# Rows of the input and output laid two neighbours to a partition, in pieces of 2 KB

## The reference, cut to what matters

```
# x: (64, 256, 256), ctx_768: (64, 120, 192), all float32
def xattn(q, kv, Wq, Wk, Wv, Wo, bo):            # 8 heads of 32
    scores = einsum('bqhd,bkhd->bhqk', heads(q @ Wq), heads(kv @ Wk)) * 32 ** -0.5
    out = einsum('bhqk,bkhd->bqhd', softmax(scores), heads(kv @ Wv))
    return out @ Wo + bo

def ffn(x, g1, b1n, w1, b1, g2, b2n, w2, b2):    # 256 -> 1024 -> 256
    h = bitlinear(layernorm(x, g1, b1n), w1, b1) # each row rounded to 8 bits by its own
    h = gelu(h)                                  # largest magnitude, weights to -1, 0, 1
    return bitlinear(layernorm(h, g2, b2n), w2, b2)

x = x + xattn(layernorm(x), ctx_768, ...)
x = x + ffn(layernorm(x), ...)
```

## Time and profile before

| What | Value |
|---|---|
| Median of three runs | 1029.75 us |
| Profiled execution, own time | 1027.94 us |
| Span of the profiled execution | 1026.3 us |
| PE busy | 919.9 us (90%) |
| DVE busy | 915.6 us (89%) |
| ACT busy | 931.9 us (91%) |
| POOL busy | 776.1 us (76%) |
| Mean granted TensorE clock | 0.977 |
| DMA packets | 276079, 146.98 MB |

### The profile page before, as it was taken

One profiled execution on the slowest core, in us unless ns is written; L12 is line 12 of the kernel. 1 busy time (PEld: TensorE's weight loads), 2 busy tenths in 40 slices (PEclk: granted clock), 3 DMA queues, 4 the chain that ended last, 5 costly groups with the idle time before them and its releaser, 6 DMA issues.

```text
span 1026.3 us, 25999 instructions
## 1 busy us (share of the span) xinstructions
PE 919.9 (90%) x7410; PEld 558.2 (54%) x7442; DVE 915.6 (89%) x1192; ACT 931.9 (91%) x2667; POOL 776.1 (76%) x1189
## 2 busy tenths in 40 slices
PE   6999999999999999999999868888888888888886
PEld 4666666666666666666666413344444444444434
DVE  2588888888888888888888899999999999999996
ACT  4789999999999999999997888999999999999993
POOL 3266665777666666666667687999999999999997
PEclk9999999999999999999999956999999999999998
DMA  6589987777866566666665333877777777777787
GB/s 171 149 158 202 185 172 164 170 158 171 173 171 153 169 163 168 162 157 175 163 161 134 94 82 69 123 125 123 121 122 121 124 120 123 121 122 123 123 124 120
DMA packets 276079, 146.98 MB, mean 143 GB/s; under 512 B 183320, under 2 KB 266520, under 8 KB 276016
## 3 DMA queue, kind: packets, MB, share of 16 engines
q1 hardware_dynamic: 258432, 129.29, 57.5%
q0 software_dynamic: 16864, 16.26, 13.3%
q10 hardware_dynamic: 720, 0.66, 0.2%
HBM read 71.62 MB, written 33.63 MB: 103 GB/s over the span
## 4 chain that ended last, share of the span: by engine, by line
PE 54%; DVE 16%; issue 14%; POOL 6%; ACT 5%; DMA 2%; SPq 1%; ACTq 1%; DVEq 0%; POOLq 0%
PE banks L1386 11%; PE banks L1377 10%; PE banks L1298 6%; PE banks L1350 6%; DVE g_max L861 6%; PE banks L1339 5%; DVE gn_low L849 4%; PE banks L1370 4%; PE banks L1360 3%; POOL nq L594 2%; DVE gn_high L849 2%; PE banks L1328 2%; PE banks L1266 2%; PE banks L1364 2%; DVE gn_high L835 2%
## 5 line engine op out<-in xcount | busy, mean ns | idle before, releaser
L1232 PE MATMUL banks<-w_t,h_t 128*128 128x512 bf16 x473 | 130.7, 399 | 81.6 <-DVE gn_low L835 39.1
L751 DVE TRANSPOSE_TENSOR_REDUCE nm_part<-banks 128x64 f16<-128x2048 f32 x64 | 147.7, 2307 | 2.6 <-PE banks L1298 2.2
L1089 ACT ACTIVATE banks<-banks,h_dq 128x1024 f32<-128x1024 f32 x128 | 141.6, 1106 | 8.3 <-PE banks L1237 6.3
L1095 ACT ACTIVATE g_dev<-banks,g_sum 128x1024 bf16<-128x1024 f32 x128 | 145.8, 1139 | 0.0
L1042 ACT ACTIVATE probs<-banks 120x512 f32<-120x512 f32 x256 | 132.2, 603 | 13.8 <-PE banks L1328 10.3
L1266 PE MATMUL banks<-w_t,g_t 128*128 128x256 bf16 x1024 | 136.8, 278 | 5.4 <-ACT h L1128 4.7
L1386 PE MATMUL banks<-wo_sb,o_t 128*128 128x256 f32 x512 | 135.2, 399 | 1.2 <-DVE xr L757 0.8
L1266 PEld LDWEIGHTS banks<-w_t,g_t 128*128 128x128 f16 x1024 | 92.8, 99 | 55.1 <-issue 39.0
L1232 PEld LDWEIGHTS banks<-w_t,h_t 128*128 (+1 forms) x504 | 48.1, 99 | 136.6 <-issue 99.1
L1377 PE MATMUL banks<-xt,wq_c 128*128 128x256 f32 x512 | 121.7, 381 | 0.0
L536 POOL COPY h_dq<-h_cl 128x2 f32<-128x2 f32 (+1 forms) x64 | 12.0, 188 | 140.8 <-DVE h_qs L814 137.8
(11 more groups left out here) (170 smaller groups left out, 2526.9 us busy)
## 6 DMA issues: line engine op xcount, KB each, us to landing
x_in<-in_x SPq DMA_DIRECT2D x64, 256.0 KB, 4.8
xt<-in_x_t SPq DMA_DIRECT2D x64, 256.0 KB, 4.1
xr<-in_x SPq DMA_DIRECT2D x64, 256.0 KB, 4.3
out<-xr SPq DMA_DIRECT2D x64, 256.0 KB, 6.0
out<-h POOLq DMA_DIRECT2D x62, 256.0 KB, 5.0
ctx_t<-in_ctx_t SPq DMA_DIRECT2D x64, 128.0 KB, 3.9
r_bc<-r_rows SPq DMA_DIRECT2D x63, 128.0 KB, 4.1
w_raw<-in_w_t SPq DMA_DIRECT2D x8, 256.0 KB, 6.1
```

The lines of the kernel that those rows point to most:

```text
L751: dve.tensor_reduce(nm_part[:, :, 0:C * RB], blocks_p, AX.X, ALU.max, negate=True, apply_transpose=True).then_inc(max_done, 1)
L1089: act.activation(u_p[t], u_p[t], ACT.Gelu, scale=h_dq[:, b, t:t + 1], accum_out=g_sum[:, p, t:t + 1]).then_inc(gelu_done, 1)
L1095: act.activation(g_dev[:, t, :], u_p[t], ACT.Square, scale=-float(F), bias=g_sum[:, p, t:t + 1], accum_out=g_ssq[:, p, t:t + 1]).then_inc( ...
L1232: pe.matmul(u_p[t][:, cols], h_t[:, b, t * C + c, :], w1_t[:, c, cols], start=(c == 0), stop=False, skip_group_check=True)
```

## The change

Five DMAs that move rows of a batch, and the host's layout of the turned input, take another order of the rows. Partition p now holds rows 2p and 2p + 1, row 2p + t in tile t. In memory these two rows are neighbours, so what was two pieces of 1 KB for a partition, 128 KB apart, is one piece of 2 KB. The turned input gives the columns in the same order. The last stores, of one tile each, still move pieces of 1 KB, now every second row.

```
-x_in[:, q, :, :] <- x[b].rearrange("(t p) n -> p t n", p=P)          # L405
+x_in[:, q, :, :] <- x[b].rearrange("(p t) n -> p t n", p=P)
-xr[:, r, :, :] <- x[b].rearrange("(t p) n -> p t n", p=P)            # L417
+xr[:, r, :, :] <- x[b].rearrange("(p t) n -> p t n", p=P)
-out[b].rearrange("(t p) n -> p t n", p=P) <- xr[:, r, :, :]          # L421
+out[b].rearrange("(p t) n -> p t n", p=P) <- xr[:, r, :, :]
-out[b].rearrange("(t p) n -> p t n", p=P)[:, t, :] <- res[...]       # L442
+out[b].rearrange("(p t) n -> p t n", p=P)[:, t, :] <- res[...]
-out[b].rearrange("(t p) n -> p t n", p=P) += res[:, r, :, :]         # L585
+out[b].rearrange("(p t) n -> p t n", p=P) += res[:, r, :, :]
...
 def laid_out(inputs):
-    a["x_t"] = a["x"].transpose(0, 2, 1).reshape(nb, d // P, P, rows).transpose(0, 2, 1, 3)
+    tiles = a["x"].reshape(nb, P, rows // P, d).transpose(0, 2, 1, 3).reshape(nb, rows, d)
+    a["x_t"] = tiles.transpose(0, 2, 1).reshape(nb, d // P, P, rows).transpose(0, 2, 1, 3)
```

More of the change, by code:

```diff
@@ L404, in attn @@
                         after(sp, x_ssq, (b - 1) * T)
-                        sp.dma_start(x_in[:, q, :, :], x[b].rearrange("(t p) n -> p t n", p=P)).then_inc(x_loaded[q], 16)
+                        sp.dma_start(x_in[:, q, :, :], x[b].rearrange("(p t) n -> p t n", p=P)).then_inc(x_loaded[q], 16)
                     b = i + 3
@@ L416, in attn @@
                         after(sp, x1_stored[r], (b - r) * 4)
-                        sp.dma_start(xr[:, r, :, :], x[b].rearrange("(t p) n -> p t n", p=P)).then_inc(xr_loaded[r], 16)
+                        sp.dma_start(xr[:, r, :, :], x[b].rearrange("(p t) n -> p t n", p=P)).then_inc(xr_loaded[r], 16)
                     b, r = i - 4, n
@@ L420, in attn @@
                         sp.wait_ge(b2_done, b + 1)
-                        sp.dma_start(out[b].rearrange("(t p) n -> p t n", p=P), xr[:, r, :, :]).then_inc(x1_stored[r], 16)
+                        sp.dma_start(out[b].rearrange("(p t) n -> p t n", p=P), xr[:, r, :, :]).then_inc(x1_stored[r], 16)
                     b = i + 3
@@ L441, in store_last @@
                     sp.wait_ge(last_out, count)
-                    sp.dma_start(out[b].rearrange("(t p) n -> p t n", p=P)[:, t, :], res[:, b % 4, t, :]).then_inc(last_stored, 16)
+                    sp.dma_start(out[b].rearrange("(p t) n -> p t n", p=P)[:, t, :], res[:, b % 4, t, :]).then_inc(last_stored, 16)
                 for n, b in enumerate((NB - 2, NB - 1)):
@@ L584, in store @@
                     pool.wait_ge(out_done, b * T + T)
-                    pool.dma_start(out[b].rearrange("(t p) n -> p t n", p=P), res[:, r, :, :],
+                    pool.dma_start(out[b].rearrange("(p t) n -> p t n", p=P), res[:, r, :, :],
                                    accum_op=ALU.add).then_inc(stored[r], 16)
```

## The result

The changed kernel takes 1033.38 us (median of 20 runs, 1029.58 to 1041.84), the kernel before on the same chip 1028.76 (20 runs): a ratio of 1.0046, 95% interval 1.0032 to 1.0060. It is slower by about 4.6 us. The forecast was 1029.0 in a range of 1025.5 to 1032.0. The profiled execution took 1033.8 us, with a span of 1032.1; rows of a profile are always of one execution.

A forecast was written before the change was run, and what follows sets the result against it. It took PE to bound the attention half and DVE the feed forward half. -0.6 (140 to 302 us) - 0.1 (start) + 0 = -0.7 us from the median 1029.75 gave 1029.05, predicted as 1029.0, range 1025.5 to 1032.

The forecast's parts named there:

- The packets: Whole kernel: packets fall from 276,079 to 243,567, of which 201,496 are under 2 KB.
- Rival 2: Whole kernel: pieces don't become 2 KB, packets stay at 276,079 and time at 1029.75 us; chance 0.06.
- What is steady: Both halves' steady parts wait for no DMA; batch periods stay at 8.75 and 6.44 us.
- rival 4: Feed forward half: adding pieces of 2 KB at 483 ns make DMA the bound, +19 us, 1049; chance 0.05.
- The adding store on POOL: Feed forward half: issue falls from 1.26 to 1.1 us, the saving turns into L619's wait for ACT; gain 0.
- The last store: Kernel end: the 3.6 us store keeps 1 KB pieces; taken as 0, bounds -0.3 to +1.4 us.
- Rival 3: Between the halves: earlier loads close PE's gaps, up to 7.6 us of clock loss goes, 1021.5; chance 0.07.
- The plain transfers: Loads and stores of rows: each lands 0.1 us sooner, bounds 0 and 0.7; counts only where a transfer sets the end.
- The start: First loads: chain passes 5.40 us through a weight load; gain 0.1 us, bounds 0 and 0.7.
- The stretch from 140 to 302 us: Attention half: 2.4 us lost in the chain through the small store; 0.6 comes back, bounds 0 and 2.4.

The follow-up runs named there:

- e1: The changed kernel again, nothing edited: 1032.29 us, ratio to the kernel before 1.0026 (1.0007 to 1.0045).
- e3: The kernel before with only the loads x_in and xr in pieces of 2 KB: 1033.77 us, ratio to the kernel before 1.0033.
- e4: The changed kernel with the small store of the deviations issued ahead of the attention store: 1031.08 us, ratio to the kernel before 1.0021.
- f1: The kernel before with x_in alone in pieces of 2 KB: 1034.50 us, ratio to the kernel before 1.0014 (0.9983 to 1.0044).
- g0: The changed kernel again, nothing edited, on another chip: 1032.57 us, ratio to the kernel before 1.0039 (1.0021 to 1.0056).
- g2: The changed kernel with the three broadcast loads behind r_bc near 24 us issued a step later: 1033.29 us, ratio to the kernel before 1.0030.
- e2: The kernel before with only the attention store to out in pieces of 2 KB: 1027.46 us, ratio to the kernel before 0.9983.
- f2: The kernel before with xr alone in pieces of 2 KB: 1033.54 us, ratio to the kernel before 0.9983 (0.9959 to 1.0006).
- f3: The changed kernel with x_in's tile padded, so its load has pieces of 1 KB: 1034.24 us, ratio to the kernel before 0.9987.
- f4: The changed kernel with x_in padded and xr loaded as two DMAs, 2 KB pieces in stores alone: 1032.64 us, ratio to the kernel before 0.9981.
- g3: The changed kernel with all loads in 1 KB and whole-batch stores in 2 KB, as f4, on another chip: 1028.95 us, ratio to before 1.0006.
- h1: The kernel before with r_bc loaded from 128 different rows of x: 1030.84 us, ratio to the kernel before 0.9963 (0.9940 to 0.9986).
- k1: The kernel before with the small store of the deviations ahead of the attention store: 1033.93 us, ratio to the kernel before 1.0007.
- k2: The changed kernel with loads in 1 KB, whole-batch stores in 2 KB, small store ahead of the attention store: 1031.97 us, ratio to before 0.9972.
- h3: The changed kernel with r_bc issued ahead of the context and the turned rows: 1078.25 us, ratio to the kernel before 1.0418.
- h4: The kernel before with r_bc issued ahead of the context and the turned rows: 1080.26 us, ratio to the kernel before 1.0444.
- g1: The changed kernel with r_bc loaded from 128 different rows of x: 1030.11 us, ratio to the kernel before 1.0014 (0.9997 to 1.0032).

## Why the prediction was wrong

*The packets*: right, 243,567 with 201,496 under 2 KB. Rival 2 is out.

*What is steady*: right. From 302 us on no batch of the attention half is longer (all start 5.4 us later than before), the feed forward half takes 1032.1 - 605.2 = 426.9 us against 426.5, and the DMA share of 0.68 instead of 0.63 cost nothing. That also puts an end to rival 4: the adding queue holds 0.124 x 16 x 1032.1 / 8928 = 229 ns for a packet, at most 258 for a data piece of 2 KB, where I took 250 and the rival needed 443.

*The adding store on POOL*: right in kind. The issue fell from 1.26 to 0.94 us (and is 0.94 in every kernel with this store in 2 KB); I took 1.1. In 300 us that saves 283.1 - 267.7 = 15.4 us of POOL, and L619's wait for ACT rose by 15.4, from 4.4 to 19.8. All of it went into the wait, as forecast. The rule cited from the Trainium skill, "DMA: Bandwidth & Descriptors", "Anatomy of one DMA — SWDGE (gpsimd) path", would have left the issue at 1.26 us. The measurement decides against it here: half as many descriptors took a quarter off.

*The last store*: right, 1028.67 to 1032.1 is 3.4 us, against 3.6.

*Rival 3*: the clock between the halves didn't recover; the first five batches there take 645.5 - 605.2 = 40.3 us against 39.8. The clock did move the time, but at 34 us, and downwards.

*The plain transfers*: this is the step that failed: "The bounds are therefore 0 and 0.7 us for each transfer". It failed twice. It bounded a larger piece only on the side of the gain, while the adding piece and the last store had got a bound on both sides. Measured by the median landing, `x_in` gained 0.1 us (4.8 to 4.7), as taken, `xr` lost 0.1 (4.3 to 4.4) and the attention store lost 0.7 (6.0 to 6.7). And it bounded the changed transfer by itself, from there to "the chain there consists of landings of 5 to 7 us which do not change themselves but wait behind x_in, xr and out. If each falls by 0.1". The landings behind them did not fall. Near 24 us `r_bc`, 1 KB for each partition like before, lands after 4.6 to 6.5 us in the seven profiled executions with `x_in` in 2 KB, the small array as source and an unchanged queue up to there (after, e1, e3, e4, f1, g0, g2), and after 2.9 to 3.8 in the nine with `x_in` in 1 KB (before, e2, f2, f3, f4, g3, h1, k1, k2). Its packets divide in the same way, 96 to 109 ns against 48 to 72. Where L413 itself was moved, it is 5.1 in h3 and 3.9 in h4, with 1 KB. (The expectation of f1 counts three late profiles and gives 3.7 for one of the others; e4 was a fourth, and the kernel before has 3.1.) The three steps overlap a little, 28.0 to 31.1 us against 27.5 to 28.5, because of e4 and k2.

So the record shows that `x_in` in 2 KB goes with the late `r_bc`, and that this costs 1.7 to 3.5 us at the start in six of seven executions and 0.5 in one. That it also takes the small array as source is shown by g1 for this place (27.5 us). Whether it is the one shared row or that it was written just before, and how it works together with the pieces of `x_in`, is not shown. It may be that with larger pieces all engines come to the shared row at the same moment; this is argued, not measured.

The start was also named in the prediction as a place where a transfer can set the end, but for its first chain link of 5.40 us, and with a gain only. DVE's idle time of 4.66 us ahead of 27.46 was there to be read: the same wait had a second releaser close behind, for `r_bc` had landed at 23.7 + 3.1 = 26.8 us, 0.7 us before DVE's start. A landing 2.7 us later could not be hidden.

*The stretch from 140 to 302 us*: forecast -0.6 us with bounds of 0 and -2.4. From the fourth batch to the end of this stretch it was +2.5 (2.9 us behind at the fourth, 5.4 at the end), of which 2.4 had come by 142.2 us before and 147.5 after, the fifteenth batch: the larger part lies before 140 us, where I had not looked; the DMA share from 85 to 190 us was 0.89 before. The mechanism was named rightly (SP's queue behind the small store), the direction wrongly. How much of these 2.5 us comes from the change stays open. Over the twelve steps from the tenth batch the changed kernel takes 4.8 us more than 12 x 8.75, the kernel before 2.1. On one chip g0 and g2, with the changed loads and the shared row, lose 6.3 and 5.8 there, g1 and g3 1.9 and 2.5, with landings of the small store up to 9.6 us in g0 and 8.0 in g1. But e1, the changed kernel again, loses 1.4, and f3 and f4, without the changed `x_in`, 6.8 and 4.5. One profiled execution of each is too few to part them.

*The range*: by its own terms, -3.1 to +1.4 on 1029.75 and 2 us each way, it runs from 1024.7 to 1033.2; the 1025.5 to 1032 stated is narrower. 1033.38 lies outside both.

## What to carry to other kernels

When a large transfer changes its shape, look at the small ones behind it which somebody waits for, and read from the trace how long each of them may be late (here `r_bc` near 24 us, 0.7 us). Give a changed transfer a bound on both sides; fewer packets for the same bytes are no gain by themselves. In a queue that is in order, count each loop that passes through a landing (landing plus the issues up to the next one) against the step of the bound engine: here 7.4 + 1.4 against 8.75 us. Two loads moved into that loop cost 4%, 1.2 us a turn by their issue and 2.1 to 2.4 us by the later landing of the small store.

## What the runs showed of the hardware beyond that

- The DMA engines' busy share at one rate (164 to 166 GB/s, 302 to 540 us) varies by more than pieces of 1 or 2 KB explain: the same kernel shows 0.67 in f4 and 0.60 in g3, and kernels with 1 KB in both loads reach 0.75 (k1). On two chips the kernels with the changed loads stand above those without: 0.67 to 0.72 (e1, e3, e4) against 0.63 (e2), and 0.64 to 0.70 (g0, g1, g2) against 0.60 (g3):

```profile
302.00:540.00 238.00, 238.00 (x2335) 162.86 (x2331) 207.68 (x356) 216.75 (x682) 156.24 (x303) 1.00 0.60 164
```

- A load of 1 KB into each of 128 partitions landed sooner from 128 different rows of the input than from the one row of the small array that had just been written: 4.0 against 5.8 us near 24 us (g1, g0), with packets of 57 against 96 ns, and the whole kernel before gained 0.37% when its `r_bc` read those rows (h1). With `x_in` in 1 KB the packets do not differ (50 ns in h1, 48 before).
- An adding piece of 2 KB costs the queue less than two of 1 KB: at most 258 ns against 2 x 138. On POOL such a DMA of 256 KB is issued in 0.94 us instead of 1.26.
- TensorE's granted clock fell to its lower level for 3.4 us after a stretch of 2 us in which PE was busy for 0.57 (after, 30 to 32 us); it fell in three of the seven executions with the late load (after, e3, g2).
